# The last steps of a graph attention layer in an order of their own on each engine

## The chip, the cores and the metric

The kernel runs on one core of one Trainium2 chip. The metric is the device time of one execution in microseconds (us); a run's time is that of the core. Engines are named TensorE (PE), VectorE (DVE), ScalarE (ACT), GpSimd (POOL) and SyncE (SP), which here only issues transfers.

## What is computed

One layer of a graph network: 3125 nodes of 128 features, 100,000 edges sorted by their destination, five edge types, eight heads of 16 features. Cut to what matters:

```python
for r in range(R):                                   # 5 edge types
    mask = edge_types == r
    q = einsum('eh,khd->ekd', x[dst], W_Q[r]); k, v = (einsum(..., x[src], W_K[r]), einsum(..., x[src], W_V[r]))
    logits = (q * k).sum(-1) / 4 + attn_bias[r]
    max_v = segment_max(where(mask, logits, -1e9), dst)
    exp_l = where(mask, exp(logits - max_v[dst]), 0)
    attn = exp_l / (segment_sum(exp_l, dst)[dst] + 1e-12)
    out += segment_sum(attn[:, :, None] * v, dst)
h = out.reshape(n, 128) @ out_proj_w.T + out_proj_b + x
out = layernorm(x + layernorm(h) * ln_gamma + ln_beta)
```

## The kernel before

**Tables first.** For each node and type the key and the value are written to a table in DRAM, and later the query as well. Then comes a stream over the edges. 512 neighbouring edges (128 partitions by 4) are a quad, and there are 196 quads. The edges are cut into three streams of 66 quads, which run side by side so that a scan works on 3 streams x 5 types x 8 heads = 120 partitions at once. Three quads, one of each stream, are a window; the windows are counted 0 to 65. The third stream has two quads less, so windows 64 and 65 have two new quads each, and a piece 66 goes over the first quads of streams 1 and 2 once more.

**One loop of steps.** Each engine runs its own copy of `for s in range(plan.steps)` (210 steps), and what it does in a step is laid down by `schedule()`. In order of the data, with the line of VectorE or of the named engine:

- GpSimd gathers key and value rows of quad m into a ring `kv` of 17 places (L1374).
- TensorE spreads the queries of quad m over its edges (`queries`, L1464, 12 matmuls in bf16).
- VectorE multiplies them with the keys (L1170) and sums over a head's features (L1192); per window it spreads the logits over the types (L1204, and L1215 for piece 66). TensorE turns them (`turn`, L1479) so that edges lie along the free axis.
- Per window VectorE scans the running maximum forward (L1254) and backward (L1269), takes the shift (L1150), ScalarE the exponential (`exp_shift`, L813; `keep_turned`, L817, keeps the last 64 columns in `carry`), VectorE scans the sums (L1293) and the totals (L1161), ScalarE takes the logarithm (L829), VectorE adds (L1240), ScalarE takes the exponential that is the attention weight (L837). The scans of window i read the results of window i-1.
- TensorE turns the weights back (`back`, L1501) into a PSUM bank. For each quad (from here on it is called a front, f) VectorE multiplies values by weights into `av` with four places (L1225) and makes the one-hot matrix `ohn` of its 32 possible nodes (L1182); TensorE sums over the edges (`collect`, L1510: four fp32 products, recorded as eight matmuls); VectorE adds the 32 columns into `aggT` (L1127). Where an `add` has a front number divisible by 8, it first loads eight registers from a table (L531).
- When all fronts of a tile of 128 nodes are in, TensorE multiplies it by the output weights (`project`, L1516), VectorE adds x (L1133), takes mean and variance (L1280, L1282), ScalarE the inverse root (L847, L849), VectorE scales (L1176), adds the features (L1196) and beta (L1232), takes the second mean and variance (L1275, L1298), and after a second root the result (L1302), which SyncE stores (L727). The 25 tiles are counted `o`; the last six, 19 to 24, are ready only after the last fronts.

Engines meet by counting semaphores: `e.wait_ge(name, n)` holds the engine's queue until the count is reached, and everything behind it on that engine waits as well. Order within a step is the same in every step: for VectorE the adds and residuals come first, then shift, totals, keys, one-hots, logits, weighing, forward and backward scan, statistics, sums, result. In the last steps the fronts are dealt out by hand:

```python
LAST_FRONTS = {186: 195, 187: 196, 188: 196, 189: 197, 190: 197, 191: 197,
               192: 199, 193: 199, 194: 200, 195: 200, 196: 201, 197: 201}
```

Of the kernel before, what the change touches and what calls it, by code (L numbers as in the profile page):

```python
# [7 lines left out]
R = 5  # L8
H = 8
D = 16  # L10
C = 128
NB = 25
# [17 lines left out]
KR = 15  # L30
# [96 lines left out]
def counts(steps):  # L127
# [8 lines left out]

VSET = counts([
    ("fd", 1), ("same", 1), ("differ", 1), ("reset", 1), ("reld", 1), ("relm", 1), ("pad", 1), ("relk", 1),
    ("n0f", 1), ("n0m", 3), ("kbm", 1), ("v1", 1), ("v2", 1), ("v3", 1), ("v3r", 1), ("wqs", 1), ("negb", 1),
    ("kvi", 1), ("keyf", 1), ("reln", 1), ("pen0", 1), ("pen1", 1), ("pen2", 1), ("sel", 1), ("pen", 1),  # L140
# [154 lines left out]
def build(nc, x_t, x_b, w_kv, w_q, w_o, params, edges, natural, firsts, out):  # L295
    ctx = ExitStack()
    with ctx:
# [9 lines left out]
        def sems(name, n):  # L307
# [11 lines left out]
        pool = sb("pool", [128, POOL])  # L319
        wq = sb("wq", [128, R, C])  # L320
# [3 lines left out]
        keyf = sb("keyf", [128, NT])  # L324
        kvi = sb("kvi", [128, NT], U32)
        reln = sb("reln", [128, NT], BF16)
# [86 lines left out]
        stq = room.take([2, R, QW])  # L413
        room = Region(pool[:, :])
# [30 lines left out]
        ohn = sb("ohn", [128, AR, 4, 32])  # L445
        LW = sb("LW", [128, 3, 4, G, H])
# [46 lines left out]
            sem("attn"), sem("nodes"), sem("weighed"), sem("collected"), sem("added"))  # L493
        projected, resid, mean1 = sem("projected"), sem("resid"), sem("mean1")
# [5 lines left out]
        plan = schedule()  # L500

# [46 lines left out]
        def bank_of(n):  # L548

            return pp[{64: 2, 65: 3, 66: 1}.get(n, 6)]  # L550
# [16 lines left out]
        def bank_in(s):  # L567

            return pp[4] if s >= NQ + 3 and s % 2 else pp[0]

        def sums_at(s, k):

            return bank_in(s)[:, 32 * k:32 * (k + 1)]

        def project_at(s, k):

            return bank_in(s)[:, 128 * (k + 1):128 * (k + 2)]

        def taken(s):

            return s - 1 if s >= NQ + 3 else s
# [200 lines left out]
        def scalar_fast(e):  # L782
# [56 lines left out]
            def root(g, k):  # L839
# [8 lines left out]
                e.wait_ge(root_log, 2 * g + k)  # L848
# [6 lines left out]
            for s in range(plan.steps):  # L855
                if s >= 1:
                    take_q(s - 1)
                if s in plan.shift:
                    exp_shift(plan.shift[s])
                    if plan.shift[s] < LASTW:  # L860
                        keep_turned(plan.shift[s])
# [8 lines left out]
                for g, k in plan.root.get(s, []):  # L870
                    root(g, k)

# [9 lines left out]
        def vector_setup(e):  # L882
# [44 lines left out]
                            est[:, 0, 0:NT].rearrange("p (q j) -> p q j", j=4),  # L927
                            n0f[:, 0:NQ, None].broadcast_to([128, NQ, 4]), ALU.subtract).then_inc(vset, 1)
# [180 lines left out]
        def vector_fast(e):  # L1109
            n0 = [e.alloc_register(f"n0{m}") for m in range(8)]  # L1110

            for s in range(plan.steps):
                o = plan.norm1.get(s)
                if o is not None:
                    y = hb[:, o % 10, :]
# [518 lines left out]
```

## Time and profile before

| | us |
|---|---|
| median of 3 runs | 1132.37 (1130.26 to 1133.01) |
| the profiled execution | 1132.2 |
| its span on the core | 1130.5 |
| VectorE busy in the span | 996.1 (88%) |
| TensorE busy in the span | 912.4 (81%) |
| last operation of VectorE ends | 1127.58 |

The span runs from the first to the last instruction of the profiled execution; its time lies 1.7 us above the span. Times in the rows below are us from the start of the span. In a timeline, idle time in front of a group stands in brackets, with what ended it; the ends of matmuls are modelled, so that two neighbours can seem to overlap.

### The profile page before, as it was taken

How to read it: one execution, taken by the hardware profiler on the slowest of the kernel's cores; microseconds unless marked ns; L12 is line 12 of the kernel's file. 1: busy time of each engine (PE TensorE's matmuls, PEld its weight loads, DVE VectorE, ACT ScalarE, POOL GpSimd, SP SyncE). 2: the span in 40 equal slices, each digit the busy share in tenths (PEclk: the TensorE clock that was granted, in tenths of full speed). 3: DMA queues.
4: the chain of work that ended last, by engine and by line, in shares of the span. 5: the costliest groups of instructions: out<-in, count | busy, mean ns of one | idle time of the engine just before them, and what ended most of it. 6: DMA issues, size and time to landing. Idle time of an engine off the chain costs nothing.

```text
span 1130.5 us, 19008 instructions
## 1 busy us (share of the span) xinstructions
PE 912.4 (81%) x5176; PEld 813.6 (72%) x5176; DVE 996.1 (88%) x1867; ACT 533.0 (47%) x977; POOL 759.0 (67%) x844
## 2 busy tenths in 40 slices
PE   6954587798889888878898977888978788887675
PEld 3523477797778787767787867788877678876665
DVE  4456798998899998999999999999989999999976
ACT  4644444555445554444554454555544344444311
POOL 0047777777777777777777777777777777777500
PEclk9976655555555555555555565556555555555555
DMA  9977667666666666656666666666676566655400
GB/s 301 368 274 220 190 207 201 181 188 191 178 191 192 174 197 192 192 169 184 193 194 190 171 186 188 192 192 181 184 198 175 144 188 174 177 175 157 139 1 13
DMA packets 120945, 209.27 MB, mean 185 GB/s; under 512 B 22797, under 2 KB 79498, under 8 KB 120606
## 3 DMA queue, kind: packets, MB, share of 16 engines
q0 software_dynamic: 37632, 102.81, 31.9%
q1 hardware_dynamic: 82194, 102.94, 29.9%
q10 hardware_dynamic: 1008, 2.25, 0.7%
q8 instruction: 45, 0.74, 0.3%
q14 instruction: 66, 0.54, 0.1%
HBM read 176.92 MB, written 30.99 MB: 184 GB/s over the span
## 4 chain that ended last, share of the span: by engine, by line
PE 34%; DVE 30%; issue 20%; DMA 7%; ACT 5%; DVEq 2%; SPq 1%; POOL 1%; ACTq 0%; POOLq 0%
PE pp L1510 10%; PE pp L1464 9%; PE pp L1501 5%; DVE pool L1254 4%; DVE av L1225 4%; DVE pool L1170 4%; DVE Tt L1161 3%; DMA qwin<-Qfast 3%; PE pp L1527 3%; PE pp L517 3%; DVE LW L1192 2%; PE LT L1479 2%; ACT pool L791 2%; DVE Mt L1269 2%; DVE pool L1150 2%
## 5 line engine op out<-in xcount | busy, mean ns | idle before, releaser
L1374 POOL DMA_INDIRECT ring<-KVtab,kvi x784 | 756.2, 965 | 305.7 <-issue 222.4
L1464 PE MATMUL pp<-qwin,pool 128*128 128x128 bf16 x2352 | 278.6, 305 | 156.2 <-ACT pool L795 85.0
L1464 PEld LDWEIGHTS pp<-qwin,pool 128*128 128x128 bf16 x2352 | 245.4, 146 | 202.9 <-ACT pool L795 111.8
L1510 PEld LDWEIGHTS pp<-ohn,av 128*128 128x128 f32 x1568 | 348.4, 326 | 32.8 <-DVE aggT L1127 32.0
L1510 PE MATMUL pp<-ohn,av 128*128 128x32 f32 x1568 | 354.0, 390 | 20.6 <-DVE aggT L1127 19.4
L1170 DVE TENSOR_TENSOR pool<-pp,ring 128x512 f32<-128x512 f32 x196 | 132.9, 678 | 41.4 <-issue 25.5
L1501 PEld LDWEIGHTS pp<-sel,pool 120*128 120x128 f32 (+1 forms) x536 | 130.3, 325 | 27.8 <-issue 26.1
L795 ACT ACTIVATE pool<-pool,one 128x512 bf16<-128x512 bf16 x196 | 141.4, 722 | 6.4
L813 ACT ACTIVATE Et<-pool 120x512 f32<-120x512 f32 (+1 forms) x66 | 41.7, 631 | 216.0 <-DVE pool L1150 216.0
L1501 PE MATMUL pp<-sel,pool 120*128 120x24 f32 (+1 forms) x536 | 130.1, 392 | 16.6 <-DVE av L1225 15.4
L791 ACT ACTIVATE pool<-rkb,npid 128x512 bf16<-128x512 bf16 x196 | 138.9, 709 | 7.9 <-PE LT L517 6.2
L1225 DVE TENSOR_TENSOR av<-ring,pp 128x512 f32<-128x512 f32 x198 | 133.6, 677 | 2.5 <-PE pp L1501 2.2
L1192 DVE TENSOR_REDUCE LW<-pool 128x32 f32<-128x512 f32 x196 | 132.8, 677 | 0.3
L829 ACT ACTIVATE Tt<-Tt,tiny 120x512 f32<-120x512 f32 (+1 forms) x66 | 47.7, 722 | 149.5 <-DVE Tt L1161 149.5
L806 ACT ACTIVATE pool<-pp 128x512 bf16<-128x512 f32 (+1 forms) x126 | 53.8, 427 | 107.6 <-PE pp L1527 70.9
L1254 DVE TENSOR_TENSOR_SCAN pool<-mk,pool,LT 120x512 f32<-120x512 bf16 x66 | 83.1, 1259 | 4.4 <-PE LT L1479 4.2
L1269 DVE TENSOR_TENSOR_SCAN Mt<-LT,pool 120x576 f32<-120x576 bf16 (+1 forms) x63 | 83.5, 1325 | 2.2
L1161 DVE TENSOR_TENSOR_SCAN Tt<-LT,pool 120x576 f32<-120x576 bf16 (+1 forms) x63 | 83.3, 1323 | 0.1
L1293 DVE TENSOR_TENSOR_SCAN pool<-LT,pool,Et 120x512 f32<-120x512 bf16 x63 | 80.3, 1275 | 0.0
L1479 PE MATMUL LT<-ident,LM 128*120 128x128 f32 (+1 forms) x268 | 69.2, 412 | 0.0
L837 ACT ACTIVATE pool<-Yt 120x512 f32<-120x512 f32 (+2 forms) x82 | 43.1, 544 | 44.1 <-DVE Yt L1240 44.1
L1127 DVE TENSOR_TENSOR aggT<-aggT,pp 128x32 f32 x196 | 34.1, 174 | 28.2 <-PE pp L1510 13.8
(121 smaller groups left out, 789.1 us busy)
## 6 DMA issues: line engine op xcount, KB each, us to landing
rkb<-Ktab SPq DMA_DIRECT2D x196, 128.0 KB
mk<-Mtab SPq DMA_DIRECT2D x201, 100.2 KB
qwin<-Qfast SPq DMA_DIRECT2D x196, 96.0 KB
KVtab<-pool SPq DMA_DIRECT2D x25, 640.0 KB, 5.3
ring<-KVtab,kvi POOLq DMA_INDIRECT x784
Qfast<-pool SPq DMA_DIRECT2D x21, 480.0 KB, 3.5
Qfast<-ring SPq DMA_DIRECT2D x4, 480.0 KB, 7.1
xs<-in_x_b SPq DMA_DIRECT2D x5, 320.0 KB, 4.6
```

The lines of the kernel that those rows point to most:

```text
L791: e.activation(ab[:, :], rkb[:, m % 3, :], ACT.Abs, bias=npid[:, 0:1]).then_inc(keys_dist, 1)
L795: e.activation(ohr[:, m % OR, :], ab[:, :], ACT.Relu, bias=one[:, 0:1], scale=-1.0).then_inc(onehot, 1)
L1161: e.tensor_tensor_scan(Tt[:, a - base:b - base][:, ::-1], total_mask(i, a, b)[:, ::-1], at_ring(Sb, i, a, b, 64)[:, ::-1], 0.0 if k == 0 e ...
L1170: e.tensor_tensor(prod[:, :].rearrange("p (j c) -> p j c", j=4), pp[2 + s % 2][:, :].rearrange("p (j c) -> p j c", j=4), kv[:, home(s), :, ...
L1192: e.tensor_reduce(LW[:, i % 3, :, g, :], prod[:, :].rearrange("p (j h d) -> p j h d", j=4, d=D), AX.X, ALU.add).then_inc(logit, 1)
L1225: e.tensor_tensor(av[:, f % AR, :].rearrange("p (j h d) -> p j h d", j=4, d=D), kv[:, home(f), :, C:2 * C].rearrange("p j (h d) -> p j h d ...
L1254: e.tensor_tensor_scan(at_ring(Fb, i, a, b, 0), mask_at(i, 0, a, b, 0), turned_at(i, a, b), at_ring(Fb, i, a - 1, a, 0) if i or k else LOW ...
L1269: e.tensor_tensor_scan(Mt[:, a - base:b - base][:, ::-1], backward_mask(i, a, b)[:, ::-1], at_ring(Fb, i, a, b, 0)[:, ::-1], LOW if k == 0 ...
L1374: e.indirect_dma_start(kv[:, home(m), j, :], None, KV, bass.IndirectOffsetOnAxis(kvi[:, 4 * q + j:4 * q + j + 1], 0)).then_inc(kv_in[m % 6 ...
L1464: last = e.matmul(pp[2 + m % 2][:, j * C:(j + 1) * C], ohr[:, m % OR, j * C:(j + 1) * C], qwin[:, m % 2, k * C:(k + 1) * C], start=(k == 0 ...
L1501: last = e.matmul(to[0:m, :, j, :], Wb[:, p:p + 4 * m].rearrange("p (n j) -> p n j", j=4)[:, :, j], sel.rearrange("p g h -> p (g h)"), sta ...
L1510: last = e.matmul(to, av[:, f % AR, j * C:(j + 1) * C], ohn[:, f % AR, j, :], start=(j == 0), stop=(j == 3))
```

## The change

Up to step 192 the steps are as before, except that `keep_turned` has a wait of its own for the shift of its window. From step 193 on no engine follows `schedule()` any more; its operations are written out one after the other.

- VectorE: the scans of windows 64 and 65 stand ahead of most of the weighing and adding of fronts 184 to 191; the norms of tiles 19 to 24 are put in between one another. The fronts 192 to 197 run in the order of `FRONT` (stream 1's three quads, then stream 2's).
- The products of fronts 183 and later go into the key half of their own place in the ring, not into `av`.
- The one-hot matrices of the last six fronts are made in the setup (`ohl`). Their room is that of `keyf`, which moves into the end of the ring (only the general path reads it).
- `sums_at` and `project_at` give the last fronts and tiles more places in PSUM (banks 0, 1, 5, 7).
- Beta is added to the features of tiles 19 to 24 by GpSimd, after its last gather; VectorE adds the sum in one instruction and has no beta pass for these tiles.
- ScalarE has the roots of the last tiles in the order `LATE_ROOTS`, and `keep_turned` ahead of `exp_shift`.

The functions that VectorE's old loop had in line (`add`, `residual`, `shift`, `total` and so on) are otherwise the same instructions.

```diff
+END = 193
+FRONT = [*range(192), 192, 194, 196, 193, 195, 197]
+IN_RING, EARLY_HOT = 183, 192
+LATE = 19
+LATE_ROOTS = [(4, 1), (4, 2), (5, 1), (6, 1), (5, 2), (6, 2), (7, 1), (8, 1), (7, 2), (9, 1), (8, 2), (9, 2)]
...
-        keyf = sb("keyf", [128, NT])
...
+        keyf = ring[:, (KR + 2) * 8 * C - NT:]
...
+        ohl = sb("ohl", [128, NQ + 2 - EARLY_HOT, 4, 32])
...
-            return pp[{64: 2, 65: 3, 66: 1}.get(n, 6)]
+            if n == 66:
+                return pp[3][:, 96:192]
+            return pp[{64: 2, 65: 3}.get(n, 6)][:, 0:96]
...
+        def sums_at(f):
+            if f < END - 11:
+                k = 0
+            elif f == END - 11:
+                return pp[1][:, 0:32]
+            else:
+                k = (f - END + 10) % 3
+            bank = pp[0] if f < END - 11 or (f - END + 10) // 3 % 2 == 0 else pp[1]
+            return bank[:, 32 * k:32 * (k + 1)]
+        def project_at(o):
+            if o < LATE:
+                k = plan.done[step_of[o]].index(o)
+                return pp[0][:, 128 * (k + 1):128 * (k + 2)]
+            return {19: pp[7][:, 0:128], 20: pp[5][:, 0:128], 21: pp[5][:, 128:256],
+                    22: pp[7][:, 128:256], 23: pp[7][:, 256:384], 24: pp[5][:, 256:384]}[o]
...
+        def hot_at(f):
+            return ohn[:, f % AR, :, :] if f < EARLY_HOT else ohl[:, f - EARLY_HOT, :, :]
+        def mark_nodes(e, f):
+            q = quad_of(FRONT[f])
+            return e.tensor_tensor(hot_at(f), reln[:, 4 * q:4 * q + 4, None].broadcast_to([128, 4, 32]),
+                                   io32[:, None, :].broadcast_to([128, 4, 32]), ALU.is_equal)
+        def weighed_at(f):
+            if f >= IN_RING:
+                return kv[:, home(FRONT[f]), :, 0:C]
+            return av[:, f % AR, :].rearrange("p (j c) -> p j c", j=4)
...
             def keep_turned(i):
+                e.wait_ge(below, SHIFT[i])
                 e.activation(carry[:, :], LT[0:GH, 448:512], ACT.Copy).then_inc(carried, 1)
...
+            keys(NQ - 1)
+            keep_turned(63)
+            exp_shift(63)
+            log_total(63)
+            exp_weigh(63)
+            keep_turned(64)
+            exp_shift(64)
+            log_total(64)
+            exp_weigh(64)
+            exp_shift(65)
+            log_total(65)
+            exp_weigh(65)
+            for g, k in LATE_ROOTS:
+                root(g, k)
...
+            for f in range(EARLY_HOT, NQ + 2):
+                mark_nodes(e, f).then_inc(vset, 1)
...
+            def weigh(f):
+                m = FRONT[f]
+                i, g = turn_of(m)
+                e.wait_ge(attn, i + 1 if i < LASTW else NW + 1)
+                if f < IN_RING:
+                    if f >= AR:
+                        e.wait_ge(collected, f - AR + 1)
+                else:
+                    e.wait_ge(logit, min(m + 1, NQ))
...
+            def with_features(o):
+                y = hb[:, o % 10, :]
+                e.wait_ge(n1_done, o + 1)
+                if o >= LATE:
+                    e.wait_ge(late_x, o - LATE + 1)
+                e.scalar_tensor_tensor(y, y, sd[:, 0, o % 10:o % 10 + 1], xs[:, plan.order[o], :], ALU.mult,
+                                       ALU.add).then_inc(g1_done, 1)
...
+            def second_stats(o):
+                if o < LATE:
+                    e.wait_ge(g2_done, o + 1)
+                else:
+                    e.wait_ge(g1_done, o + 1)
...
+            shift(63)
+            times_key(193)
+            one_hot(183)
+            logits(193)
+            masked(64)
+            weigh(183)
+            e.wait_ge(collected, 182)
+            add(181)
+            sums(63)
+            times_key(194)
+            one_hot(184)
+            logits(194)
+            total(63)
+            weigh(184)
+            forward(64)
+            norm_sum(63)
+            one_hot(185)
+            weigh(185)
+            times_key(195)
+            logits(195)
+            backward(64)
+            shift(64)
+            masked(65)
+            masked_again()
+            e.wait_ge(collected, 183)
+            add(182)
+            one_hot(186)
+            sums(64)
+            one_hot(187)
+            total(64)
+            weigh(186)
+            weigh(187)
+            one_hot(188)
+            weigh(188)
+            norm_sum(64)
+            forward(65)
+            e.wait_ge(collected, 186)
+            add(183)
+            add(184)
+            add(185)
+            one_hot(189)
+            one_hot(190)
+            backward(65)
+            shift(65)
+            weigh(189)
+            weigh(190)
+            weigh(191)
+            one_hot(191)
+            sums(65)
+            total(65)
+            e.wait_ge(collected, 189)
+            add(186)
+            add(187)
+            add(188)
+            norm_sum(65)
+            e.wait_ge(collected, 192)
+            add(189)
+            add(190)
+            add(191)
+            e.wait_ge(projected, 20)
+            residual(19)
+            first_stats(19)
+            e.wait_ge(projected, 22)
+            residual(20)
+            residual(21)
+            scaled(19)
+            with_features(19)
+            weigh(192)
+            second_stats(19)
+            second_mean(19)
+            first_stats(20)
+            first_stats(21)
+            result(19)
+            scaled(20)
+            with_features(20)
+            weigh(193)
+            weigh(194)
+            second_stats(20)
+            second_mean(20)
+            scaled(21)
+            with_features(21)
+            result(20)
+            second_stats(21)
+            second_mean(21)
+            weigh(195)
+            weigh(196)
+            result(21)
+            e.wait_ge(collected, 195)
+            add(192)
+            add(193)
+            add(194)
+            weigh(197)
+            e.wait_ge(projected, 24)
+            residual(22)
+            residual(23)
+            first_stats(22)
+            first_stats(23)
+            scaled(22)
+            scaled(23)
+            with_features(22)
+            second_stats(22)
+            second_mean(22)
+            e.wait_ge(collected, 198)
+            add(195)
+            add(196)
+            add(197)
+            with_features(23)
+            result(22)
+            e.wait_ge(projected, 25)
+            residual(24)
+            first_stats(24)
+            second_stats(23)
+            second_mean(23)
+            scaled(24)
+            with_features(24)
+            second_stats(24)
+            second_mean(24)
+            result(23)
+            result(24)
...
+            def with_beta(o):
+                e.wait_ge(resid, o + 1)
+                x = xs[:, plan.order[o], :]
+                e.tensor_tensor(x, x, beb2[:, :], ALU.add).then_inc(late_x, 1)
+            for o in range(LATE, NB):
+                with_beta(o)
...
+            queries(194)
+            e.wait_ge(qcut, 6 * len(LATER_Q))
+            collect(182)
+            queries(195)
+            turn(64, 128)
+            e.wait_ge(added, 182)
+            collect(183)
+            collect(184)
+            back(62)
+            turn(65, 128)
+            collect(185)
+            turn(66, 16)
+            e.wait_ge(added, 183)
+            collect(186)
+            collect(187)
+            back(63)
+            collect(188)
+            e.wait_ge(added, 186)
+            collect(189)
+            collect(190)
+            collect(191)
+            e.wait_ge(added, 189)
+            e.wait_ge(full_sum, TOTAL[63])
+            project(19)
+            e.wait_ge(added, 192)
+            e.wait_ge(below, SHIFT[LASTW])
+            project(20)
+            project(21)
+            back(64)
+            back(65)
+            back(66)
+            collect(192)
+            collect(193)
+            collect(194)
+            collect(195)
+            e.wait_ge(added, 195)
+            e.wait_ge(resid, 20)
+            project(22)
+            project(23)
+            collect(196)
+            collect(197)
+            e.wait_ge(added, 198)
+            e.wait_ge(resid, 22)
+            project(24)
```

## Rows read from the trace of the kernel before

**Rows 1.** Windows: length, busy us of PE, PEld, DVE, ACT, POOL, granted clock, DMA share, GB/s.
```profile
1000.00:1060.00 60.00, 45.86 (x269) 42.87 (x268) 57.54 (x117) 26.48 (x47) 45.67 (x48) 0.50 0.60 171
...
1070.00:1080.00 10.00, 5.28 (x24) 4.82 (x24) 7.68 (x15) 0.74 (x2) 0.00 (x0) 0.50 0.00 0
...
1100.00:1110.00 10.00, 10.00 (x53) 9.88 (x52) 6.54 (x23) 0.99 (x4) 0.00 (x0) 0.50 0.01 3
...
1120.00:1130.50 10.50, 0.00 (x0) 0.00 (x0) 4.96 (x19) 2.27 (x10) 0.00 (x0) 0.50 0.07 20
```

**Rows 2.** Waits from 1053 to the end: us in total, times, longest.
```profile
PE pp L1510 <- DVE aggT L1127: 8.8, 4, 4.7
```

**Rows 3.** Timeline of VectorE, step 193 to the last chunk: start, us, line, shapes.
```profile
1060.53 0.31 DVE L1150 SCALAR_TENSOR_TENSOR pool<-Mt,clamp,carry 120x64 f32<-120x64 f32 x1
...
1078.70 0.69 DVE L1225 TENSOR_TENSOR av<-ring,pp 128x512 f32<-128x512 f32 x1 [2.21 <-PE pp L1501]
...
1090.24 0.29 DVE L1182 TENSOR_TENSOR ohn<-reln,io 128x128 f32<-128x128 bf16 x1 [0.52 <-PE pp L1510]
...
1097.65 0.89 DVE L1240 TENSOR_TENSOR Yt<-pool,Tt 120x704 f32<-120x704 f32 x1 [0.95 <-ACT Tt L829]
...
1100.61 0.83 DVE L1127 TENSOR_TENSOR aggT<-aggT,pp 128x32 f32 x3 [1.65 <-PE pp L1510]
...
1101.61 0.49 DVE L1182 TENSOR_TENSOR ohn<-reln,io 128x128 f32<-128x128 bf16 x2
...
1110.01 0.51 DVE L1127 TENSOR_TENSOR aggT<-aggT,pp 128x32 f32 x2 [1.01 <-issue]
```

**Rows 4.** Timeline of PE over the last fronts (one collect is eight of these).
```profile
1095.02 5.30 PE L1510 MATMUL pp<-ohn,av 128*128 128x32 f32 x24 [2.53 <-DVE aggT L1127]
...
1100.13 4.32 PE L1501 MATMUL pp<-sel,pool 120*128 120x24 f32 x24
...
1104.38 1.22 PE L1516 MATMUL LT<-woT,aggT 128*128 128x128 f32 x4
...
1105.40 3.46 PE L1510 MATMUL pp<-ohn,av 128*128 128x32 f32 x16
...
1112.29 3.60 PE L1510 MATMUL pp<-ohn,av 128*128 128x32 f32 x16
```

**Rows 5.** Timeline of VectorE, the last tiles' norms.
```profile
1118.51 0.49 DVE L1133 TENSOR_TENSOR hb<-LT,xs 128x128 f32<-128x128 f32 x2 [0.33 <-PE LT L1516]
...
1122.40 0.35 DVE L1176 SCALAR_TENSOR_TENSOR hb<-hb,mv,small 128x128 f32<-128x128 f32 x1 [1.02 <-ACT sd L849]
...
1122.79 0.35 DVE L1196 SCALAR_TENSOR_TENSOR hb<-hb,sd,xs 128x128 f32<-128x128 f32 x1
...
1123.18 0.29 DVE L1232 TENSOR_TENSOR hb<-hb,beb 128x128 f32<-128x128 f32 x1
...
1123.50 0.29 DVE L1275 BATCH_NORM_STATS2 st<-hb 128x6 f32<-128x128 f32 x1
...
1123.83 0.18 DVE L1298 BATCH_NORM_AGGREGATE mv<-st 128x2 f32<-128x6 f32 x1
...
1127.23 0.35 DVE L1302 TENSOR_SCALAR hb<-hb,mv,sd 128x128 f32<-128x128 f32 x1 [0.37 <-ACT sd L849]
```

**Rows 6.** Timeline of ScalarE: window 63, and a root of the end.
```profile
1061.47 0.63 ACT L813 ACTIVATE Et<-pool 120x512 f32<-120x512 f32 x1 [5.02 <-DVE pool L1150]
...
1062.00 0.21 ACT L817 ACTIVATE carry<-LT 120x64 f32<-120x64 f32 x1
...
1098.58 0.79 ACT L837 ACTIVATE pool<-Yt 120x704 f32<-120x704 f32 x1 [0.96 <-DVE Yt L1240]
...
1124.05 0.29 ACT L847 ACTIVATE sd<-mv,epst 128x1 f32<-128x1 f32 x1 [1.68 <-DVE mv L1298]
...
1124.37 0.20 ACT L849 ACTIVATE sd<-sd 128x1 f32<-128x1 f32 x1
```

**Rows 7.** Timeline of GpSimd's setup: an elementwise pass over 128x128.
```profile
1.27 0.28 POOL L1317 TENSOR_SCALAR_AFFINE_SELECT ident<-ident 128x128 f32<-128x128 f32 x1 [0.24 <-POOL ident L1315]
```

**Rows 8.** Timeline of VectorE in the setup, its long wait.
```profile
66.42 0.69 DVE L973 COPY pool<-pp 128x512 f32<-128x512 f32 x1 [21.67 <-PE pp L517]
```

More of the change, by code:

```diff
@@ L500, in build @@
         plan = schedule()
+        step_of = {o: k for k, v in plan.done.items() for o in v}
         def group(o):
@@ L854, in scalar_fast @@
             keys(1)
-            for s in range(plan.steps):
+            for s in range(END):
                 if s >= 1:
@@ L1110, in vector_fast, with add, residual @@
             n0 = [e.alloc_register(f"n0{m}") for m in range(8)]
-            for s in range(plan.steps):
+            def add(f):
+                m = FRONT[f]
+                lo, hi = (1, 32) if m in (1, 2) else (0, 1) if m >= NQ else (0, 32)
+                to = aggT[:, bass.ds(window(e, n0, n0m, m, 1, NQ + 2), 32)][:, lo:hi]
+                if f:
+                    e.wait_ge(added, f)
+                e.tensor_tensor(to, to, sums_at(f)[:, lo:hi], ALU.add).then_inc(added, 1)
+            def residual(o):
+                if o >= 10:
+                    e.wait_ge(n2_done, o - 9)
+                    e.wait_ge(out_put[o % 10], 16 * (o // 10))
+                e.tensor_tensor(hb[:, o % 10, :], project_at(o), xs[:, plan.order[o], :], ALU.add).then_inc(resid, 1)
@@ L1113, in vector_fast @@
+            for s in range(END):
                 o = plan.norm1.get(s)
-                if o is not None:
-                    y = hb[:, o % 10, :]
                 if s - 2 in plan.fronts or s - 1 in plan.done:
@@ L1120, in vector_fast @@
                     e.wait_ge(collected, fronts_until(s - 2))
-                for k, f in enumerate(plan.fronts.get(s - 2, [])):
-                    lo, hi = (1, 32) if f in (1, 2) else (0, 1) if f >= NQ else (0, 32)
-                    to = aggT[:, bass.ds(window(e, n0, n0m, f, 1, NQ + 2), 32)][:, lo:hi]
-                    if f:
-                        e.wait_ge(added, f)
-                    e.tensor_tensor(to, to, sums_at(s - 1, k)[:, lo:hi], ALU.add).then_inc(added, 1)
-                for k, d in enumerate(plan.done.get(s - 1, [])):
+                for f in plan.fronts.get(s - 2, []):
+                    add(f)
@@ L1129, in vector_fast @@
+                for d in plan.done.get(s - 1, []):
                     e.wait_ge(x_ready, len(X_ADD))
-                    if d >= 10:
-                        e.wait_ge(n2_done, d - 9)
-                        e.wait_ge(out_put[d % 10], 16 * (d // 10))
-                    e.tensor_tensor(hb[:, d % 10, :], project_at(s - 1, k), xs[:, plan.order[d], :], ALU.add).then_inc(resid, 1)
+                    residual(d)
                 if s in X_ADD:
-                    k = X_ADD[s]
-                    e.wait_ge(xb_in[k], 16)
@@ L1194, in vector_fast @@
+                logits(s)
                 if o is not None:
-                    e.wait_ge(n1_done, o + 1)
-                    e.scalar_tensor_tensor(y, y, sd[:, 0, o % 10:o % 10 + 1], xs[:, plan.order[o], :], ALU.mult,
-                                           ALU.add).then_inc(g1_done, 1)
+                    with_features(o)
                 if s + 1 in plan.turn:
-                    i = plan.turn[s + 1]
-                    last = quads_until(i)
-                    e.wait_ge(logit, last)
@@ L1257, in vector_fast @@
[L1257 to L1272 removed]
+                    norm_sum(plan.total[s])
```

376 lines of the change are left out of this document (194 added, 182 removed).

## The prediction

> **What bounds the kernel now.** I read the windows of time first, then the waits, then the timelines of the last 70 us. In the long middle VectorE is the bound: busy 57.5 of 60 us, with TensorE at 46 [rows 1]. The change leaves that stretch alone. From about 1060, where step 193 begins, it is different: in 1070 to 1080 VectorE is busy 7.7 and TensorE 5.3 of 10 us, in 1100 to 1110 TensorE is busy all the time and VectorE 6.5, and in the last 10.5 us TensorE does nothing and VectorE 5.0 [rows 1]. So no engine is full; the order in which they hand work to one another sets the time. Four times, for 8.8 us in sum, a `collect` waits for an `add` of VectorE [rows 2]: the longest, 4.7 us, because `add(183)` stands behind the two scans of window 64 while TensorE may not reuse the bank. VectorE in its turn waits 2.21, 0.52 and 0.95 us before its last `norm_sum` [rows 3]. Everything after 1100 is one chain: three `back`s, four `project`s' worth, six collects [rows 4], then the last tiles' norms, one tile after the other [rows 5]. TensorE's granted clock is 0.50 (the 1.2 GHz level) in all four stretches [rows 1], in those where it idles too, and I let it stay there.
>
> **How the change is costed.** I walk the new order with the durations of these rows, each operation starting when its engine is free and what it waits for is done. From the rows: a pass over 512 columns holds VectorE 0.60 us, a 128-column one-hot 0.20, a scan of 512 or 576 columns 1.2 to 1.3, a pass that needs the one before it starts 0.03 after its end; an `add` 0.12, or 0.3 with another behind it (three in 0.83 [rows 3]); a `collect` 1.76 (three in 5.30), three `back`s 4.3, a `project` 0.6 (two tiles' worth of four matmuls in 1.22) [rows 4]. The same walk over the order of before ends at 1127.7, where the trace has 1127.58, so its own error there is 0.1 us; for an order never seen I allow 1.5.
>
> *To the last norm_sum.* VectorE's instructions from 1060.4 on are the same ones, in another order. Before it reaches `norm_sum(65)` at 1097.65 with 3.68 us of idle time [rows 3]. In the new order the scans of window 64 and 65 don't meet a wait: TensorE has two collects and `back(62)` out of the way during the scans, and 185 needs no free place in `av`. Left are two waits: the register load ahead of `add(184)`, which was hidden behind a scan and now stands between two adds (the same load in the open costs 1.01 to 1.1 [rows 3]; here a scan piece covers part of it: 0.63), and 0.3 for the logarithm, behind which the adds 186 to 188 now stand. The residual of tile 19 (0.2) goes behind the `norm_sum`. 3.68 + 0.2 - 0.9 = 3.0; with the gaps between dependent pairs counted one by one the walk gives 3.2: `norm_sum(65)` at 1094.5.
>
> *To the last collect.* Its weights take ScalarE 0.79 [rows 6]. Three adds (0.9) and `project` 20 and 21 (1.1) follow, and TensorE starts `back(64)` at 1097.3, before 1100.13: 2.8 sooner. The two projects, which stood behind the backs, are done by then, so the collects of fronts 192 and on begin at 1101.6, before 1105.4 [rows 4]: 3.8 sooner. Then the new order gives some back: after four collects TensorE projects tiles 22 and 23 and for that waits for the adds 192 to 194; these wait for `collect(194)` (done 1107.1) and then for the register load, 1.1 in the open, so they end at 1109.0. TensorE idles 0.5, projects 1.1, and only then has collects 196 and 197 (3.7). They end at 1114.0, before 1115.9 (1112.29 + 3.60 [rows 4]): 1.9 sooner. The six one-hots that went to the setup are not on this path.
>
> *To the end.* Before: from 1115.9 to 1127.58, 11.7 us, because tiles 22, 23 and 24 go through two roots each, one after the other; a tile takes 2.6 to 3.3, as from 1122.40 on, with 1.02 and 0.37 of waits for ScalarE [rows 5]. New: tiles 22 and 23 do most of theirs while TensorE collects 196 and 197. What remains after 1114.0: three adds 0.9, `project(24)` and its way 0.8, residual 0.33, two statistics passes 0.33 and 0.21 with tile 23's second ones in between, a root 0.3 + 0.2 with its ways [rows 6], scaling 0.39, features 0.39, statistics 0.33 and 0.21, a root 0.55, the result 0.35 [rows 5]: 5.4 us with the small waits between, ending at 1119.4. Three beta passes of 0.33 are among the 6.3 us that this saves.
>
> Sum: 1.9 + 6.3 = 8.2 us. The store of the last tile and what follows it (1127.58 to 1130.5, 2.9) is unchanged: both last results come 0.7 apart, as before. The profiled execution took 1132.2 with a span of 1130.5; 8.2 less is a span of 1122.3 and a time of 1124.0. The median shown, 1132.37, is 0.2 above the profiled execution, so I forecast 1124.2.
>
> **The parts costed at nothing.** *Beta on GpSimd:* no row has an elementwise pass of two inputs there. Nearest are an elementwise pass with one input, 0.28 [rows 7], and VectorE's beta pass, 0.29 [rows 5]; I take 0.4, with 0.28 and twice that as bounds. It is hidden by tile 24's statistics, root and scaling, 1.5 us between residual and features; GpSimd has no gathers left by then (busy 0.00 from 1070 on [rows 1]). Without this cover each microsecond more would be one more at the end. The GPSIMD Engine Reference of the Trainium skill (section 4.1, Engine selection) speaks against the move: two-input elementwise work belongs on VectorE, GpSimd being about twice as slow. By that rule a pass takes an estimated 0.6 us, which is hidden all the same, so the sum would be equal; no row here shows it. *Six one-hots in the setup:* 0.2 each (two in 0.49 [rows 3]), with the wait for `reln` 1.3 us, in front of 21.67 us in which VectorE waits for TensorE [rows 8]; 1.3 if that cover were gone. *The ring instead of `av`:* the same pass and the same products, other addresses; at nothing, with 0.1 us for each of 15 fronts as the bound above. *The wait in `keep_turned`:* it waits for passes that `exp_shift` in front of it has already waited for. The copy starts 0.1 before the exponential ends [rows 6], so the wait is read in its shadow; bounds 0 and, should it break the overlap, 0.1 for each of 63 windows, 6 us if ScalarE were on the path every time. With VectorE at 96% [rows 1] it is not; I take 0.
>
> **Rivals.**
> *The middle gives less.* In the walk VectorE reaches the adds that TensorE waits for with only tenths to spare in several places. If the three register and bank hand-overs (adds 182, 184, 192) cost a microsecond each more than I gave them, the 1.9 us are lost and the end still wins 6.3: 1126.1. For it: TensorE idles about 10 us in the new walk too, so any slip goes through.
> *GpSimd is late.* From 1.5 us per pass on it decides; at 3 us, for tiles 22 to 24 in turn, the end is 3.9 later: 1128.1. Against it: 0.28 [rows 7].
> *GpSimd and VectorE get in each other's way.* If a pass of VectorE with two inputs in SBUF (the features, 0.35) takes twice as long beside GpSimd's pass, three of them on the path make 1.0: 1125.2. Against it: the weighing passes are 0.68 to 0.69 with gathers running or not. It is what the same reference says under Key points (8): the SBUF interfaces are shared, with contention where VectorE's instruction has two SBUF inputs; no elementwise pass of GpSimd in the stream is in this trace to test it.
> *Nothing comes out.* The end shortens but the middle, undone by a stall of 4 us or so that I don't see (VectorE queued behind a `wait_ge` for a collect which itself waits behind a `back`), takes it all back, or the changed places in SBUF slow the stream by 0.7%: about 1132.
> *Slower.* The wait in `keep_turned` recurs in every window. If it costs as much as the copy itself (0.2 [rows 6]) and lies on the path all 63 times, that is 12.6 us: 1124.2 + 12.6 = 1136.8. It makes the kernel slower from 0.13 us per window on. For it: it is the one edit that repeats. Against it: the rows' overlap, and VectorE's share.
>
> **Chances and range.** The forecast 0.62; less in the middle 0.16; the two about GpSimd 0.07 together; nothing comes out 0.10; slower 0.05. About 0.3% (3.4 us) is what a measurement of this kernel can tell from no change; the runs shown lie 2.75 us apart. Faster by more than that means below 1129.0, and the first three cases do: 0.85, plus 0.01 of the fourth. Same 0.10, slower 0.04. The forecast's own range is 1.5 for the walk and 1.4 for the runs, about 1122 to 1126.5; up to the second and third case, and with the bounds of the ring and the wait, 1121.3 to 1128.3.
>
> **What would show it.** Right: `norm_sum(65)` near 1094.5, the first of the three backs near 1097.3, the last collect ending near 1114, 5 to 6 us from there to the last result; in the waits, collects waiting for adds some 5 us in sum, not 8.8; GpSimd's six passes under 0.6 us, each over before its features pass. Wrong: a span of 1060 to 1094 that isn't 3 us shorter (the middle); more than 6 us after the last collect (GpSimd, or the roots' order); a start of step 193 later than 1061 (the wait, the setup). The forecast fails most easily in what an idle TensorE or a blocked queue adds to each hand-over, which the walk takes from an order with fewer of them.

## The result, and the profile after

The changed kernel takes 1128.73 us (median of 20 runs) against 1132.84 us before (20 runs): ratio 0.9962, 95% interval 0.9953 to 0.9972, so 3.2 to 5.3 us less, in the middle 4.1. Forecast were 8.2, with 1128.3 as the upper end of the range. It is faster, but by half of what was forecast, and its median lies above that end.

The profiled execution has a span of 1127.2 us, before 1130.5. Where the forecast 8.2 went can be read from two distances. The first is from the shift of window 63, the first pass of the rewritten part, to VectorE's last result. Before it is 1060.53 to 1127.58 [rows 3, 5], 67.05 us. The timeline of VectorE after, the rows that answer to [rows 3]:

```profile
1061.87 0.28 DVE L1202 SCALAR_TENSOR_TENSOR pool<-Mt,clamp,carry 120x64 f32<-120x64 f32 x1
...
1085.85 0.51 DVE L1179 TENSOR_TENSOR aggT<-aggT,pp 128x32 f32 x2 [0.96 <-DVE aggT L1179]
...
1096.16 0.89 DVE L1288 TENSOR_TENSOR Yt<-pool,Tt 120x704 f32<-120x704 f32 x1 [0.23 <-ACT Tt L871]
...
1109.37 0.79 DVE L1179 TENSOR_TENSOR aggT<-aggT,pp 128x32 f32 x3 [1.17 <-issue]
...
1120.27 0.34 DVE L1377 TENSOR_SCALAR hb<-hb,mv,sd 128x128 f32<-128x128 f32 x1 [0.37 <-ACT sd L891]
```

From 1061.87 to 1120.61 it is 58.74 us: 8.31 less, as forecast. The waits of 2.21 and 0.52 in front of VectorE's passes are gone; the only idle times that the view marks up to the last `norm_sum` are the register load's 0.96 and 0.23 for the logarithm. TensorE's timeline after, answering to [rows 4]:

```profile
1098.86 4.18 PE L1752 MATMUL pp<-sel,pool 120*128 120x24 f32 x24
1102.97 7.04 PE L1764 MATMUL pp<-ohl,ring 128*128 128x32 f32 x32
1110.22 1.22 PE L1770 MATMUL LT<-woT,aggT 128*128 128x128 f32 x4 [0.22 <-DVE aggT L1179]
1111.23 3.46 PE L1764 MATMUL pp<-ohl,ring 128*128 128x32 f32 x16
1116.12 0.80 PE L1770 MATMUL LT<-woT,aggT 128*128 128x128 f32 x2 [1.42 <-DVE aggT L1179]
```

Three backs, four collects, the projects of tiles 22 and 23, two collects, the last project; the last collect ends at 1114.69. The 8.8 us in which collects waited for an `add` [rows 2] are gone (the prediction had about 5 left). What TensorE still waits for adds stands in front of the projects:

```profile
PE LT L1770 <- DVE aggT L1179: 3.1, 4, 1.4
```

The second distance is from the last result to the end of the span: 2.9 us before, 6.6 after (1120.61 to 1127.2). No engine computes in these 6.6 us. The instructions of the line that closes the kernel (`with ctx:`), first those of the kernel before, then those of the changed one; each row has the engine's queue, the operation, its duration in ns (least, median, most) and its first and last start:

```profile
L297 POOLq DRAIN  x1: 21000/21000/21000, 1053.8 to 1053.8; - x1
L297 PEldq DRAIN  x1: 1220/1220/1220, 1117.3 to 1117.3; - x1
L297 DVEq DRAIN  x1: 386/386/386, 1127.2 to 1127.2; - x1
L297 SPq COMPARE_BRANCH  x1: 38/38/38, 1130.1 to 1130.1; - x1
```
```profile
L313 PEldq DRAIN  x1: 847/847/847, 1116.1 to 1116.1; - x1
L313 POOLq DRAIN  x1: 9725/9725/9725, 1117.3 to 1117.3; - x1
L313 ACTq DRAIN  x1: 233/233/233, 1120.0 to 1120.0; - x1
L313 DVEq DRAIN  x1: 386/386/386, 1120.3 to 1120.3; - x1
L313 SPq COMPARE_BRANCH  x1: 38/38/38, 1123.1 to 1123.1; - x1
...
L313 SPq EVENT_SEMAPHORE  x1: 17/17/17, 1127.2 to 1127.2; - x1
```

```profile
1098.11 0.45 POOL L1626 TENSOR_TENSOR xs<-xs,beb 128x128 f32<-128x128 f32 x1 [31.93 <-DVE hb L1185]
1099.47 0.93 POOL L1626 TENSOR_TENSOR xs<-xs,beb 128x128 f32<-128x128 f32 x2 [0.91 <-DVE hb L1185]
1111.85 0.86 POOL L1626 TENSOR_TENSOR xs<-xs,beb 128x128 f32<-128x128 f32 x2 [11.45 <-DVE hb L1185]
1117.32 0.45 POOL L1626 TENSOR_TENSOR xs<-xs,beb 128x128 f32<-128x128 f32 x1 [4.61 <-DVE hb L1185]
```

Its last pass ends at 1117.77, the drain 9.3 us later. The waits of SyncE's queue put the 4 us down to another engine:

```profile
SPq L768 <- DVE hb L1377: 11.4, 3, 8.2
SPq L313 <- PEq L313: 3.9, 1, 3.9
SPq L774 <- DMA out<-hb: 1.1, 1, 1.1
```

TensorE's queue, which it names, had drained by 1116.95. So there were two readings to tell apart: A, GpSimd's drain holds the end; B, TensorE's end does. A third, C, was that the missing part lies in the stream ahead of step 193: window 63's shift begins 1.34 us later in the trace of the changed kernel.

### The profile page after: what moved, and what is told of

It is laid out like the page before. It is cut to its first block, busy times and chain, and to the rows that moved or that the text cites. A ratio compares the mean times of both kernels' runs of the same rounds, so it can differ in the third digit from the quotient of the medians.

```text
span 1127.2 us, 19020 instructions
## 1 busy us (share of the span) xinstructions
PE 907.7 (81%) x5176; PEld 808.0 (72%) x5176; DVE 995.2 (88%) x1861; ACT 533.2 (47%) x977; POOL 762.6 (68%) x850
## 4 chain that ended last, share of the span: by engine, by line
DVE 33%; PE 23%; issue 23%; DMA 9%; ACT 4%; POOL 4%; DVEq 2%; SPq 0%; ACTq 0%; POOLq 0%
PE pp L1764 7%; PE pp L1717 7%; DVE pool L1302 5%; DVE av L1276 4%; DVE pool L1224 4%; POOL ring L1618 4%; DMA ring<-KVtab,kvi 4%; DVE Tt L1214 3%; PE pp L1752 3%; DVE LW L1236 3%; PE pp L538 3%; DVE pool L1202 2%; DMA qwin<-Qfast 2%; PE pp L1782 2%; DVE pool L1331 2%
## 5 line engine op out<-in xcount | busy, mean ns | idle before, releaser
L1764 PEld LDWEIGHTS pp<-ohn,av 128*128 128x128 f32 x1464 | 321.1, 322 | 22.2 <-DVE aggT L1179 21.6
L1764 PE MATMUL pp<-ohn,av 128*128 128x32 f32 x1464 | 326.3, 386 | 11.0 <-DVE aggT L1179 9.2
L1276 DVE TENSOR_TENSOR av<-ring,pp 128x512 f32<-128x512 f32 x183 | 123.8, 677 | 0.0
L1782 PE MATMUL pp<-wq,xqT 128*128 128x512 f32 (+1 forms) x84 | 57.8, 790 | 0.0
```

Of the source, the lines that this page charges most:

```text
L1276: e.tensor_tensor(weighed_at(f).rearrange("p j (h d) -> p j h d", d=D), kv[:, home(m), :, C:2 * C].rearrange("p j (h d) -> p j h d", d=D), ...
L1764: last = e.matmul(sums_at(f), weighed_at(f)[:, j, :], hot_at(f)[:, j, :], start=(j == 0), stop=(j == 3))
```

## The experiments

e1 to e11 ran on chips on which the stream is slower (the kernel before takes 1315 to 1331 us there). The part from step 193 on of the same kernel agrees to a tenth on every chip on which it ran, so the two distances, each read from one trace, decide, and the ratios, each against the kernel before on the same chip, stand beside them. Single runs of one kernel spread by 10 us, so the medians don't resolve 1 us, and the times of e8, e9 and e12, one run each, show nothing by themselves.

| run | this, us | before, us | ratio (95%) | window 63's shift to last result | behind it |
|---|---|---|---|---|---|
| before | | | | 67.05 | 2.9 |
| changed | 1128.73 | 1132.84 | 0.9962 (0.9953 to 0.9972) | 58.74 | 6.6 |
| e1 beta on VectorE | 1320.96 | 1331.44 | 0.9931 (0.9904 to 0.9958) | 59.35 | 2.9 |
| e2 beta early | 1321.81 | 1331.44 | 0.9939 (0.9917 to 0.9961) | 59.23 | 2.9 |
| e3 before, late GpSimd | 1338.01 | 1331.44 | 1.006 (1.0035 to 1.0085) | 67.04 | 8.9 |
| e4 changed | 1312.01 | 1314.55 | 0.9993 (0.9976 to 1.0009) | 58.77 | 6.7 |
| e5 beta early | 1306.40 | 1314.55 | 0.9946 (0.9925 to 0.9967) | 59.19 | 2.9 |
| e6 and no keep wait | 1309.10 | 1314.55 | 0.9955 (0.9935 to 0.9975) | 58.77 | 2.9 |
| e7 and loads early | 1307.70 | 1314.55 | 0.9947 (0.9929 to 0.9964) | 57.80 | 2.9 |
| e8 norms not between | 1318.11 | 1330.09 | one run | 61.92 | 2.9 |
| e9 products in av | 1321.03 | 1330.09 | one run | 58.76 | 2.9 |
| e10 changed | 1325.05 | 1330.09 | 0.9966 (0.9946 to 0.9987) | 58.76 | 6.6 |
| e11 as e7 | 1320.72 | 1330.09 | 0.9918 (0.9890 to 0.9946) | 57.90 | 2.9 |
| e12 before, beta on GpSimd | 1131.48 | 1134.70 | one run each | 66.65 | 2.9 |

**e1: beta back on VectorE**

```diff
             with_features(19)
+            with_beta(19)
...
-            for o in range(LATE, NB):
-                with_beta(o)
```

The same line stands behind each of the other five features passes; the loop taken out is GpSimd's.

> The new orders kept, but beta is added by VectorE again (a pass behind each features pass of tiles 19 to 24) and GpSimd does nothing after its last gather. Theory A (GpSimd's closing drain: in the changed kernel it begins at 1117.3 and takes 9.7 us, and ends last): the end is no longer GpSimd's, so the span is that of VectorE's last result plus 2.9 us; the result is later by two or three beta passes of 0.33, at about 1121.5, the span about 1124.4, the ratio to before 0.994. Theory B (TensorE's end holds the last barrier, as the wait's label has it): the span stays at 1127. Theory C (the missing 4 us are in the stream before step 193, where the setup and the extra wait of keep_turned make it later): the span rises by the beta passes, to 1128.

Measured: 59.35 to the last result, 0.61 more than with GpSimd's help, and 2.94 behind it. In sum 3.0 us less than the changed kernel. The three beta passes cost 0.6 and not 1.0: tile 23's stands where VectorE waits 0.33 for `project(24)` in the changed kernel, and a part of tile 22's where it waits 0.17 for the collects. Theory B (TensorE) and C (the stream) would both have kept the 6.6.

**e2: beta early on GpSimd**

```diff
+        def late_at(o):
+            return wq[:, o - LATE, :] if o < NB - 1 else xqT[:, 0, :]
...
-                e.wait_ge(resid, o + 1)
-                x = xs[:, plan.order[o], :]
-                e.tensor_tensor(x, x, beb2[:, :], ALU.add).then_inc(late_x, 1)
+                e.tensor_tensor(late_at(o), xs[:, plan.order[o], :], beb2[:, :], ALU.add).then_inc(late_x, 1)
+            e.wait_ge(vset, VSET["beb2"])
+            e.wait_ge(x_ready, len(X_ADD))
+            e.wait_ge(qcut, 6 * len(LATER_Q))
```

> GpSimd adds beta to the features of tiles 19 to 24 right after its last gather, into room that is free by then, without waiting for the residuals; VectorE is as in the changed kernel. Theory A (drain): the six passes are over at about 1069, the drain at about 1078, and the end is VectorE's again: last result near 1120.6, span 1123.5, 3.7 us less than the changed kernel, ratio to before about 0.993. Theories B (TensorE's end) and C (the stream): the span stays at 1127, ratio 0.996.

The same six passes, only 38 to 55 us earlier, counted from window 63's shift: 2.9 behind the last result. What costs is therefore not that GpSimd does the work but when it does it last. The way to the last result is 0.5 longer than in the changed kernel. VectorE's timeline of e2 and, below it, GpSimd's show why:

```profile
1257.06 0.73 DVE L1205 SCALAR_TENSOR_TENSOR pool<-Mt,clamp,carry 120x64 f32<-120x64 f32 x1
1257.72 0.67 DVE L1205 SCALAR_TENSOR_TENSOR pool<-Mt,clamp,LT 120x448 f32<-120x448 f32 x1
```
```profile
1255.61 2.10 POOL L1628 TENSOR_TENSOR wq<-xs,beb 128x128 f32<-128x128 f32 x5
1257.68 0.44 POOL L1628 TENSOR_TENSOR xqT<-xs,beb 128x128 f32<-128x128 f32 x1
```

The first piece of the shift takes 0.73 us, not 0.28, which makes up the difference. It reads two tensors in SBUF while GpSimd runs; the second piece reads one of its two from PSUM (`LT`) and is as fast as ever.

**e3: one more column for GpSimd, late, in the kernel before**

```diff
+            e.wait_ge(n2_done, NB - 1)
+            e.memset(pid[:, :], 0.0).then_inc(tick, 1)
```

> The kernel before with one more instruction: GpSimd sets a column of 128x1 (not used any more) once the result of tile 23 is there, at about 1126.9. Theory A (drain ends some 9.3 us after GpSimd's last instruction, whatever that is): the span grows from 1130.5 to about 1136.4, ratio 1.005. If the drain only belongs to two-input passes, or by theories B and C: no change, 1130.5.

Measured: the median is 6.6 us higher (ratio 1.0035 to 1.0085), and 8.9 instead of 2.9 stand behind the last result, 6.0 more (expected 5.9). The timeline of GpSimd and the closing line:

```profile
1325.96 0.10 POOL L1378 MEMSET pid<- 128x1 f32 x1 [70.16 <-DVE hb L1302]
```
```profile
L297 POOLq DRAIN  x1: 9358/9358/9358, 1325.9 to 1325.9; - x1
```

A pass of 0.1 us, and the drain ends 9.2 us after it. It is the same after a gather, after a pass with two inputs and after a memset, so among these three kinds the kind of instruction doesn't matter. This run makes the drain the cause: put into the kernel before, a late instruction alone does the damage.

**e4 and e5: the changed kernel and beta early side by side**

> The changed kernel once more, on the chip of the runs beside it, for the comparison with them. By the drain theory its span ends 9.3 us after GpSimd's last pass, 6.6 us after VectorE's last result; ratio to before 0.996 to 0.997.

> Beta early on GpSimd once more, beside the changed kernel on one chip. Drain theory: the time from window 63's shift to the last result stays that of the changed kernel (58.7) or 0.45 longer, where a pass of VectorE with two SBUF inputs meets GpSimd's passes; the rest after the last result is 2.9, not 6.6; so some 3.3 us less than the changed kernel. Stream theory: no difference between the two.

The distances come out as expected. The medians lie 5.6 apart (3.3 were expected), e4's ratio is nearer to 1 than in the other two comparisons of the changed kernel, and its interval (0.9976 to 1.0009) includes 1: on this chip the change as it stands shows no gain in time.

**e6: keep_turned without its new wait**

```diff
             def keep_turned(i):
-                e.wait_ge(below, SHIFT[i])
+                if i >= 63:
+                    e.wait_ge(below, SHIFT[i])
```

> Beta early, and keep_turned has its new wait only from window 63 on (before that exp_shift in front of it has waited for the same). If the wait costs nothing, as I had it: the time of beta early. If it costs 0.01 to 0.02 us in each of 63 windows on the path (what would make step 193 begin 1.3 us later, as in the one trace of the changed kernel): about 1 us less.

Median 1309.1 against 1306.4 with the wait: nothing is gained by leaving it out. On this chip that excludes a cost of several us, not one of 1 us.

**e7: the two register loads early**

```diff
+            def preload(m):
+                regs = n1 if m == 184 else n2
+                e.load(regs, n0m[0:1, m:m + len(regs)])
...
             sums(64)
+            preload(184)
             one_hot(187)
...
             total(65)
+            preload(192)
```

> Beta early, and the two register loads in front of add(184) and add(192) are done sooner, behind the scans sums(64) and total(65), into registers of their own. The waits of 0.96 and 1.17 us before these adds in the changed kernel go. The first lies in front of the last scans, so everything behind it is 0.9 sooner; of the second only TensorE's 0.22 us wait before project 22 is won, and perhaps what follows. From window 63's shift to the last result: 59.2 less about 1.1. If the load only moves its stall (the queue isn't far enough ahead of VectorE): no change or slower.

57.80, which is 1.4 less than e5. Of these, 0.3 is the first piece of the shift, which takes 0.38 here and 0.70 in e5, so the early loads are worth 1.1, as expected. The medians (1307.70, e5 1306.40) don't show it. VectorE's waits before the two groups of adds, in e7:

```profile
1268.67 0.51 DVE L1194 TENSOR_TENSOR aggT<-aggT,pp 128x32 f32 x2 [0.33 <-DVE aggT L1194]
...
1291.35 0.79 DVE L1194 TENSOR_TENSOR aggT<-aggT,pp 128x32 f32 x3 [0.32 <-PE pp L1783]
```

0.33 and 0.32 us, not 0.96 and 1.17. The second group now waits for its collects and not for the queue.

**e8: the norms of tiles 22 and 23 not between the collects**

```diff
             residual(23)
-            first_stats(22)
...
-            second_mean(22)
             e.wait_ge(collected, 198)
             add(195)
             add(196)
             add(197)
+            first_stats(22)
...
+            second_mean(22)
```

> Beta early, and the norms of tiles 22 and 23 (statistics, scaling, features, second statistics of 22) stand behind the adds 195 to 197 and not beside the collects 196 and 197. If the end's gain comes from putting the norms between one another, as in my sum, the walk gives 2.65 us more from window 63's shift to the last result: 61.4 to 61.8, against 58.8 to 59.2. If the gain came from fewer passes or the shorter PSUM hand-overs: no difference.

61.92. The first piece of the shift met GpSimd's passes here and took 0.83, so 0.55 of it belongs to that; without it 61.4 is 2.6 more than e6 and e9 (58.77 and 58.76), whose shift met none. The walk had 2.65. Putting the norms beside the collects thus carries a little under half of the 5.8 us that the end wins, and the beta passes 0.6 (e1); the rest is not taken apart. VectorE's timeline has the lengthened shift and the hole in which the norms stood:

```profile
1251.55 0.83 DVE L1205 SCALAR_TENSOR_TENSOR pool<-Mt,clamp,carry 120x64 f32<-120x64 f32 x1
...
1305.16 0.80 DVE L1182 TENSOR_TENSOR aggT<-aggT,pp 128x32 f32 x3 [2.95 <-PE pp L1769]
```

**e9: products in av**

```diff
-IN_RING, EARLY_HOT = 183, 192
+IN_RING, EARLY_HOT = 198, 192
```

> Beta early, and the products of fronts 183 and later go into the four places of av again, each waiting for the collect four fronts before it. By the walk no wait appears in this order: 58.8 to 59.2 from window 63's shift to the last result, the ring brings nothing by itself. If the ring is what takes VectorE's waits away: 1 to 3 us more.

58.76, and e6 with the ring has 58.77: the ring brings nothing by itself, as the walk had it.

**e10 and e11: the changed kernel and the best version side by side**

> The changed kernel a third time, beside the version with early beta and loads on one chip: 58.7 us from window 63's shift to the last result, 6.6 us behind it.

> Beta early and both register loads early once more, beside the changed kernel on one chip: 57.8 us from window 63's shift to the last result, 2.9 behind it, in sum 4.7 less than the changed kernel and 9.2 less than before, if the stream before step 193 is the same in all three.

The best version (e7's kernel) is 9.4 us faster than before (9.2 expected) and 4.3 faster than the changed kernel (4.7 expected); its ratio to before is 0.9890 to 0.9946, that of the changed kernel 0.9946 to 0.9987, so the two intervals only meet. On the chip of e4 and e7 the same two kernels also lie 4.3 apart (1312.01 and 1307.70).

**e12: beta on GpSimd alone, in the kernel before**

```diff
                 if o is not None:
                     e.wait_ge(n1_done, o + 1)
+                    if o >= 19:
+                        e.wait_ge(late_x, o - 18)
...
-                if o is not None:
+                if o is not None and o < 19:
                     e.wait_ge(g1_done, o + 1)
                     e.tensor_tensor(y, y, beb2[:, :], ALU.add).then_inc(g2_done, 1)
...
+            for o in range(19, NB):
+                e.wait_ge(resid, o + 1)
+                x = xs[:, plan.order[o], :]
+                e.tensor_tensor(x, x, beb2[:, :], ALU.add).then_inc(late_x, 1)
```

> The kernel before with one part of the change alone: GpSimd adds beta to the features of tiles 19 to 24 once their residual is taken, VectorE has no beta pass for them. Three beta passes of 0.33 leave the chain of tiles 22 to 24: from window 63's shift to the last result 66.1, not 67.05, or 0.2 to 0.4 more where the scaling pass (two SBUF inputs) meets GpSimd's pass. GpSimd's last pass ends about 0.9 us after the last residuals, 7 us ahead of the last result; a drain of 9.3 us then ends about when the store does, so 2.9 to 3.3 us stand behind the last result, not 6.6. If the pass itself, not its distance from the end, made the changed kernel's 6.6: 6.6 here too.

66.65 and 2.9: of the 0.55 above 66.1, 0.3 are two passes of tile 22 lengthened beside GpSimd, and 0.3 came earlier in the same way (both below). GpSimd's last pass ends at 1119.67 here, 7.1 us ahead of the last result, and the drain (9.99 us from 1118.9) ends at 1128.9, within the time of the last store. So the drain behind the same six passes costs nothing in the old order and 3.7 us in the new one, whose last result follows the last pass after 2.8 us. VectorE's timeline beside two pairs of GpSimd's passes (1105.66 to 1106.57 and 1118.76 to 1119.67), then TensorE's:

```profile
1105.70 1.03 DVE L1183 TENSOR_TENSOR ohn<-reln,io 128x128 f32<-128x128 bf16 x2
...
1118.80 0.56 DVE L1177 SCALAR_TENSOR_TENSOR hb<-hb,mv,small 128x128 f32<-128x128 f32 x1
1119.40 0.42 DVE L1199 SCALAR_TENSOR_TENSOR hb<-hb,sd,xs 128x128 f32<-128x128 f32 x1
...
1122.64 0.35 DVE L1199 SCALAR_TENSOR_TENSOR hb<-hb,sd,xs 128x128 f32<-128x128 f32 x1
```
```profile
1112.18 3.59 PE L1520 MATMUL pp<-ohn,av 128*128 128x32 f32 x16 [0.26 <-DVE av L1228]
```

Scaling and features take 0.56 and 0.42 us instead of 0.35 each. Two one-hots take 1.03 instead of the 0.48 of before, the weighing behind them is late, and TensorE waits 0.26 ahead of its last two collects, where before it doesn't wait.

## Why the prediction was wrong

**The step that failed** is the one that took what follows the last result over unchanged: "The store of the last tile and what follows it (1127.58 to 1130.5, 2.9) is unchanged". It asked what the last store needs and not which engine closes the program last. The part costed at nothing, "*Beta on GpSimd*", fails with it: its cover of 1.5 us is right for the pass (0.45 us, taken at 0.4), but behind the pass stands a drain that ends 9.3 us later, and the drain's cover is the time from the last pass to the end of the span, 2.8 + 2.9 = 5.7 us. 9.3 - 5.7 = 3.6 us are missing, and 3.7 were measured. The trace of before has the row: the drain's 21 us from 1053.8 end 9.2 us after the last gather (1065.58). The prediction went by busy times, in which a drain doesn't count. My rival "GpSimd is late" had the right engine and the wrong mechanism: it put the delay in front of the features pass, with 1.5 us per pass as the point from which it decides.

**To the last norm_sum**: right. From window 63's shift it was forecast at 34.0 us (1060.5 to 1094.5) and is 34.3, before 37.1. The load ahead of `add(184)` stands open for 0.96 instead of 0.63. That the new order of the scans brings the 2.8 us is read from the timelines; of its parts only the load (e7) and the ring (e9) have a run of their own, and the new places in PSUM have none.

**To the last collect**: right in kind, and 0.6 better than forecast: the collects end 2.5 sooner after the shift than before, forecast 1.9. `back(64)` begins 37.0 after the shift (forecast 36.8), the last collect ends 52.8 after it (forecast 53.5). The give-back was smaller than the walk had it, in part since TensorE waits 0.22 for the adds 192 to 194 and not 0.5, in part since the last two collects take 3.5 and not 3.7.

**To the end**: 5.9 us from the last collect to the last result, forecast 5.4, before 11.7: a gain of 5.8, forecast 6.3. That the norms beside the collects carry 2.6 of it is shown by e8. Altogether 58.74 us, in the walk 58.9 (1060.5 to 1119.4); the gain 8.31, forecast 8.2. That the sum is so close is partly luck: 0.6 more in the middle and 0.5 less at the end cancel.

**The middle gives less**: this rival didn't come true. Its price was too low by its own condition: three hand-overs of a microsecond each would take up to 3.0 us, not 1.9, and make 1127.2.

**The ring, the one-hots, the wait**: the ring is nothing (e9), as forecast. No cost of the setup or of the wait is seen either. The shift of window 58, first before and then after:

```profile
983.00 0.28 DVE L1150 SCALAR_TENSOR_TENSOR pool<-Mt,clamp,carry 120x64 f32<-120x64 f32 x1
```
```profile
982.20 0.28 DVE L1202 SCALAR_TENSOR_TENSOR pool<-Mt,clamp,carry 120x64 f32<-120x64 f32 x1
...
1008.93 0.69 DVE L1224 TENSOR_TENSOR pool<-pp,ring 128x512 f32<-128x512 f32 x1 [2.20 <-issue]
```

Up to there the shifts of the changed kernel begin 0.9 us earlier on average (between 2.3 earlier and 0.15 later), and those of e12, whose stream is that of before, 0.8 earlier, so this is the difference between two executions. The 1.34 us arise in windows 59 and 60, most of them in one wait of 2.20 us where the trace of before has 0.49; they set off the sign of being wrong, a step 193 later than 1061. Whether they have to do with the change stays open. The medians over 20 runs (4.1) against the two distances (8.31 - 3.67 = 4.64) leave 0.5 us for it, within the interval.

**GpSimd and VectorE in each other's way**: right in kind, not in place. These passes of the changed kernel stand beside two of GpSimd's:

```profile
1099.51 0.57 DVE L1346 SCALAR_TENSOR_TENSOR hb<-hb,mv,small 128x128 f32<-128x128 f32 x1
1100.11 0.43 DVE L1353 SCALAR_TENSOR_TENSOR hb<-hb,sd,xs 128x128 f32<-128x128 f32 x1
1100.77 0.69 DVE L1276 TENSOR_TENSOR ring<-ring,pp 128x512 f32<-128x512 f32 x1 [0.23 <-PE pp L1752]
```

Scaling and features of tile 19 take 0.57 and 0.43, but behind them VectorE waits for a `back` all the same; for tiles 22 to 24 GpSimd's passes meet statistics, which read one tensor and keep their 0.29. The prediction's evidence against this rival was no evidence: the weighing pass, 0.68 with gathers or without, reads one of its tensors from PSUM. The trace agrees with the Trainium skill's GPSIMD Engine Reference, Key points: contention where VectorE's instruction has two SBUF inputs.

## What to carry to other kernels

An engine's last instruction has a closing cost of its own, and it differs by engine: before giving an idle engine work near the end, read the DRAIN rows of the line that closes the kernel, and count from its last instruction, whatever it is. Here work for GpSimd is free until an estimated 6.4 us before the last result (9.3 - 2.9), and from there on each microsecond later is one more: ending 7.1 us before it cost nothing (e12), 2.8 before it 3.7 us (the changed kernel), 0.6 before it 6.0 us (e3). A tail that is shortened brings such fixed closings to the surface, so a gain there must be summed per engine up to the end of the span, not up to the last result.

## What the runs showed of the hardware

- GpSimd's closing drain ends 9.2 to 9.3 us after its last instruction: after a gather (before), after a two-input pass (changed, e4, e10) and after a memset of one column (e3). VectorE's, ScalarE's and TensorE's end within 0.1 us of their engine's last operation; they last 0.39, 0.23 and 0.85 to 1.2 us.
- A pass of VectorE with two tensors in SBUF takes longer while GpSimd runs an elementwise pass: 0.73 instead of 0.28 us (e2), 0.56 and 0.42 instead of 0.35 (e12). With one of the tensors in PSUM (the second piece of the shift, 0.67 in e2), or with one tensor only (statistics, 0.29), it doesn't. Gathers on GpSimd don't do it: the features pass, with two tensors in SBUF, takes 0.34 to 0.35 us in all 25 tiles of the kernel before, of which 19 run beside a gather, wholly or in part:

```profile
L1196 DVE SCALAR_TENSOR_TENSOR hb<-hb,sd,xs x25: 336/341/352, 483.4 to 1125.4; 128x128 f32<-128x128 f32 x25
```

- A load of eight registers in VectorE's queue in front of an `add` leaves VectorE idle for 0.96 and 1.17 us (the changed kernel). Placed behind a scan it leaves 0.33 (e7).
- The wait shown for SyncE at the end of the changed kernel names TensorE's queue, which had drained 10 us before the end; the drain that did end last was GpSimd's.
